# A mixture-of-experts first layer on TensorE: float32r operands in two parts in place of bf16 operands in three

## The chip, the core and the metric

The kernel runs on one core of a Trainium2 chip. The metric is the device time of one execution in microseconds (us), as the median of several executions. The core has TensorE (matrix products into PSUM banks), VectorE, ScalarE (activations), GpSimd and SyncE, which issues the DMAs here. Each runs its own program; they meet only at semaphores.

## The reference, cut to what matters

Eight batches of 1056 tokens (1024 image tokens and 32 text tokens) of width 64 go through a tokenizer, one attention block and one feed-forward block. Only the last concerns the change. It takes the normed tokens `x` and adds, over eight experts, a gated two-layer network:

```python
def step(acc, params):
    w1, bb1, w2, bb2, we = params
    h = jax.nn.gelu(xf @ w1 + bb1, approximate=False)
    y = h @ w2 + bb2
    return (acc + we[:, None] * y, None)
out, _ = jax.lax.scan(step, jnp.zeros_like(xf), (W1, b1, W2, b2, cw.T))
```

`W1` is 8 x 64 x 128, `W2` is 8 x 128 x 64, and `cw` holds the two largest softmax gates of each token and zero for the other experts. The inputs and the result are fp32.

## The kernel before, in words

The program has two phases. Phase 1 does the tokenizer and the attention, one batch in each "slot", with the steps of neighbouring batches placed beside a slot's 99 attention units (`run_phase1`). Batches go in four pairs; a tile of 128 partitions holds the 64 channels of both batches of a pair. Phase 2 (`run_phase2`, from line 1142 on) is the feed-forward block. It goes over four pairs, in each over two batches, three chunks of 352 tokens (`chunk[c]`) and four pairs of experts (`k`): 24 steps for each pair of batches, 96 in all. The order is written out by hand, the same for all engines.

The first layer has to keep more of the mantissa than bf16 holds, so both operands are cut into three bf16 parts, and six products of parts are summed. A contraction is over 64 channels only, so two parts are stacked on the 128 partitions and one matmul does two products. `w01`, `w10`, `w20` are the weights' stacks, `x01` and `x02` those of the tokens. One expert and chunk is three matmuls of 128 rows x 128 columns on 352 tokens (line 1329). They go into one of the banks 0 to 3.

In a step, TensorE does this: it waits for the gelu that frees the bank, does the three matmuls of two experts (`product`, six matmuls), and then the second layer of the step before it (`experts_out`, line 1317): two fp32 matmuls of 128 rows x 64 columns on 352 tokens, one into the lower and one into the upper half of bank 4 or 5. The trace shows each fp32 matmul as two pairs of a weight load and a matmul. ScalarE does the two gelus (line 1285), VectorE multiplies the result with the gates (line 1304), GpSimd adds up (lines 1267 and 1273). After some of the steps, TensorE also does one of the norm's steps of the next pair (`AT_NORM`: lines 613, 436, 472, 624 and, after VectorE has chosen the gates, the transposes of line 630), and the fold of a finished batch (line 1347).

The three parts of the tokens are made once for each pair, among the norm's steps: part 0 is ScalarE's copy (line 508), then VectorE subtracts (line 583), casts (line 586) and subtracts again (line 589). These three stand in VectorE's order at steps 10, 11 and 12, between the operations that choose the gates (`CHOOSE`, lines 516 to 536, three at each of the steps 10 to 15). SyncE copies the parts to the stacks with four DMAs for each batch (`stack`, line 1213), ahead of the gates' DMAs for the first batch (`load_gates`, line 1220).

The weights' parts are made by seven VectorE operations in the last attention slot, at the units `AT_SPLIT` (lines 968 to 981). In phase 1 the tokens' parts share their tiles with the parts of queries and keys (`qk_part`).

Of the kernel before, what the change touches and what calls it, by code (L numbers as in the profile page):

```python
# [4 lines left out]

F32 = mybir.dt.float32
BF16 = mybir.dt.bfloat16
I32 = mybir.dt.int32
ALU = mybir.AluOpType
ACT = mybir.ActivationFunctionType  # L10
# [51 lines left out]
X_EARLY = 14  # L62
AT_LOAD = {"first": [2 + 3 * k for k in range(X_DMAS - X_EARLY)], "load": [30 + 3 * k for k in range(X_DMAS)]}
AT_FFN = 60
AT_SPLIT = [4, 10, 16, 22, 28, 34, 40]

def max_order():

# [50 lines left out]
def build(nc, x, txt, tok_w, w_qkv, w_proj, b_proj, gate_w, gate_b, w1, b1, w2, b2, consts, out):  # L119
    with ExitStack() as ctx:  # L120
# [26 lines left out]
        gate_sb = sb("gate_sb", [P, E])  # L147
        gate_bias = sb("gate_bias", [P, E])
        w1_sb = sb("w1_sb", [P, E, HID])
        w01, w10, w20 = [sb(name, [P, E, HID], BF16) for name in ("w01", "w10", "w20")]  # L150
        w2_sb = sb("w2_sb", [P, E, D])
        biases = sb("biases", [P, E + E // 2])
        b1_sb, b2_sb = biases[:, 0:E], biases[:, E:E + E // 2]
# [9 lines left out]
        roots = sb("roots", [P, 2 * KT + 2])  # L163
        root_work = sb("root_work", [P, 2, 2 * KT + 2])

        qk_part = x_part = [sb(f"part{i}", [P, L], BF16) for i in range(3)]
        x_rest = sq

        TILES = 2 * KT + 2
        gate_pair = sb("gate_pair", [P, 2, E])  # L170
# [153 lines left out]

        FIRST_NORM = {57: [("centre", 0)], 59: [("centre", 1)], 61: [("centre", 2)], 64: [("roots", 0)],
                      67: [("scale", 0)], 69: [("scale", 1)], 71: [("scale", 2)], 74: [("gates", 0)],
                      76: [("split", 0), ("choose", 0)], 79: [("split", 1), ("choose", 1)],
                      82: [("split", 2), ("choose", 2)], 84: [("choose", 3)], 86: [("choose", 4)],
                      88: [("choose", 5)], 92: [("turn", 0)]}


# [142 lines left out]
                                            ident[0:n, 0:n], start=True, stop=True)  # L474
            return last

        X_STACKS = 4
        KPB = NCH * E
        YPB = KPB // 2
        NORM_FILLS = 2 * NCH + 3  # L480
# [14 lines left out]
        def norm_scalar(act, name, i, p):  # L495
            if name == "centre":
                if i == 0:
                    at_least(act, x_split, 3 * p)
                act.wait_ge(norm_full, NORM_FILLS * p + i + 1)
                src = norm_bank(p, i)[:, 0:CH]  # L500
                nc.scalar.activation(xc[:, chunk[i]], src, ACT.Copy)
                nc.scalar.activation(sq[:, chunk[i]], src, ACT.Square).then_inc(norm_read, 1)
            elif name == "gates":

                act.wait_ge(norm_read, NORM_FILLS * p + GATES)
                for stacks in x_stacked:
                    at_least(act, stacks, 16 * X_STACKS * p)
                nc.scalar.activation(x_part[0][:, :], xn[:, :], ACT.Copy).then_inc(x_part0, 1)
            elif (name, i) == ("choose", 1):
                act.wait_ge(gate_step, CHOICE * p + 2)  # L510
                nc.scalar.activation(gate_e[:, :, :], gate_e[:, :, :], ACT.Exp).then_inc(gate_exp, 1)
# [27 lines left out]
        def norm_vector(dve, name, i, p):  # L539
# [12 lines left out]
            elif name == "scale":  # L552
                fill, tokens = ROOTS + 1 + i, wide[i]
                dve.wait_ge(norm_full, NORM_FILLS * p + fill + 1)
                v.tensor_tensor(xn[:, tokens], xc[:, tokens],
                                norm_bank(p, fill)[:, 0:tokens.stop - tokens.start], ALU.mult)\
                  .then_inc(norm_read, 1)
            elif name == "gates":
                dve.wait_ge(norm_full, NORM_FILLS * p + GATES + 1)
                bank = norm_bank(p, GATES)  # L560
                for bp in range(2):
                    v.tensor_tensor(logits[:, KT * bp:KT * bp + KT, :],
                                    bank[:, 0:P].rearrange("p (t b e) -> p b t e", b=2, e=E)[:, bp],
                                    gate_bias[:, :].unsqueeze(1).broadcast_to([P, KT, E]), ALU.add)
                v.tensor_tensor(logits[0:TXT, 2 * KT:TILES, :],
                                bank[0:TXT, P:P + 2 * E].rearrange("p (b e) -> p b e", e=E),
                                gate_bias[0:TXT, :].unsqueeze(1).broadcast_to([TXT, 2, E]), ALU.add)\
                  .then_inc(norm_read, 1)
            elif name == "choose":

                if i == 0:
                    dve.wait_ge(norm_read, NORM_FILLS * p + GATES + 1)
                for j in range(3 * i, min(3 * i + 3, CHOICE)):
                    if j > 0:
                        dve.wait_ge(gate_step, CHOICE * p + j)
                    if j == 13:
                        dve.wait_ge(gate_exp, p + 1)
                    CHOOSE[j]().then_inc(gate_step, 1)
            elif name == "split":

                if i == 0:
                    dve.wait_ge(x_part0, p + 1)
                    ins = v.tensor_tensor(x_rest[:, :], xn[:, :], x_part[0][:, :], ALU.subtract)  # L583
                elif i == 1:
                    dve.wait_ge(x_split, 3 * p + 1)
                    ins = v.tensor_copy(x_part[1][:, :], x_rest[:, :])
                else:
                    dve.wait_ge(x_split, 3 * p + 2)
                    ins = v.tensor_tensor(x_part[2][:, :], x_rest[:, :], x_part[1][:, :], ALU.subtract)  # L589
                ins.then_inc(x_split, 1)  # L590
            elif name == "turn":

                dve.wait_ge(norm_full, NORM_FILLS * p + TURN + 1)
                at_least(dve, cw_stored, 16 * 3 * p)
                bank = norm_bank(p, TURN)
                v.tensor_copy(cw_t[:, :], bank[:, 0:P])
                v.tensor_copy(cw_tail[:, :], bank[0:2 * E, P:P + TXT]).then_inc(norm_read, 1)
# [79 lines left out]
        with nc.Block() as block:  # L677
# [173 lines left out]
            def _(dve):  # L851
# [106 lines left out]
                def attend_unit(b, par, u, g):  # L958
# [1 line left out]
                        return  # L960


                    rest = qk_rest[:, 0:E * HID].rearrange("p (e n) -> p e n", e=E)
                    low, high = slice(0, D), slice(D, P)
                    v = nc.vector
                    step = AT_SPLIT.index(u)
                    at_least(dve, w_split, step)
                    if step == 0:
                        ins = v.tensor_copy(w01[:, :, :], w1_sb[:, :, :])
                    elif step == 1:  # L970
                        ins = v.tensor_tensor(rest, w1_sb[:, :, :], w01[:, :, :], ALU.subtract)
                    elif step == 2:
                        ins = v.tensor_copy(w10[:, :, :], rest)
                    elif step == 3:
                        ins = v.tensor_tensor(w20[low, :, :], rest[low], w10[low, :, :], ALU.subtract)
                    elif step == 4:
                        ins = v.tensor_copy(w20[high, :, :], w01[high, :, :])
                    elif step == 5:
                        ins = v.tensor_copy(w01[high, :, :], w10[high, :, :])
# [8 lines left out]
            def _(pe):  # L988
# [68 lines left out]
                def side(stage, i, t, par, pair, g):  # L1057
# [100 lines left out]

        x01 = sb("x01", [P, B, L], BF16)
        x02 = sb("x02", [P, B, L], BF16)
# [9 lines left out]

        AT_NORM = {0: [("centre", 0)], 1: [("centre", 1)], 2: [("centre", 2)],
                   3: [("roots", 0)], 5: [("scale", 0)], 6: [("scale", 1)], 7: [("scale", 2)], 9: [("gates", 0)],
                   10: [("split", 0), ("choose", 0)], 11: [("split", 1), ("choose", 1)],
                   12: [("split", 2), ("choose", 2)], 13: [("choose", 3)], 14: [("choose", 4)], 15: [("choose", 5)],
                   16: [("turn", 0)]}

        FOLD_LAST, FOLD_FIRST = 8, 20
# [25 lines left out]
        with nc.Block() as block:  # L1205
            @block.sync
            def _(sp):
                def stack(b):

                    sp.wait_ge(x_split, 3 * (b // 2) + 3)  # L1210
# [99 lines left out]
            def _(pe):  # L1310
# [10 lines left out]
                def product(b, bp, c, k, n):  # L1321
                    if (c, k) == (0, 0):
                        pe.wait_ge(x_stacked[bp], 16 * X_STACKS * (n + 1))
                        if isinstance(b, int) and b == 0:
                            pe.wait_ge(w_split, 7)
# [71 lines left out]
```

## Time and profile before

| | us |
|---|---|
| Median of 3 executions (lowest to highest) | 1002.04 (996.79 to 1002.44) |
| The profiled execution, by the device's clock | 1001.97 |
| Its span from the first to the last instruction | 1000.2 |
| Phase 2, from its first matmul at 763.78 to the end | 236.4 |

The span is 1.8 us shorter than the profiled execution's time, which lies within 0.1 us of the median. Times inside the profile count from the span's start. A matmul's record runs until its result has left the array, some time after the next one may start, so what a matmul costs in a row of them is the distance between starts. "PE" rows are matmuls, "PEld" rows are the loads of the stationary operand. A shape of 64\*128 on such a row is rows (contraction) by columns of the stationary operand.

### The profile page before, as it was taken

What the parts mean: (1) busy time and instruction counts of PE and PEld (TensorE: products, weight loads), DVE (VectorE), ACT (ScalarE), POOL (GpSimd) and SP (SyncE); (2) the same over time, 40 slices, a digit from 0 to 9 for tenths busy, and PEclk for the clock granted to TensorE, in tenths of its full rate; (3) what the DMA queues carried; (4) which work ended last, traced back from release to release, by engine and by line L of the source; (5) the groups of instructions that cost most, each with busy time, mean ns of one, the idle gap of its engine ahead of it and who ended that gap; (6) DMA issues with size and microseconds to landing.
All of it is one profiled execution on the core that took longest, in us unless ns stands there. A gap on an engine that the chain in (4) does not pass through costs nothing. (4 is left out here: it accounts for less than half of the span.)

```text
span 1000.2 us, 17890 instructions
## 1 busy us (share of the span) xinstructions
PE 899.0 (90%) x5900; PEld 374.9 (37%) x5900; DVE 573.0 (57%) x1201; ACT 494.4 (49%) x1189; POOL 138.7 (14%) x148
## 2 busy tenths in 40 slices
PE   5665899999999989999999999999965989899996
PEld 5241322433342343343243334333412535354443
DVE  4025565578874557876557887788230553636331
ACT  0020254466664536665446676666533454555552
POOL 0010100011010011101001101001000344444443
PEclk9965589899999988999989999999876999999998
DMA  8329351027551005536002305100006655382731
GB/s 153 57 47 163 62 62 31 3 35 119 97 69 44 2 4 67 117 67 110 2 1 30 40 2 68 44 3 1 1 5 141 120 126 117 80 184 52 155 78 22
DMA packets 55864, 64.58 MB, mean 65 GB/s; under 512 B 23893, under 2 KB 41825, under 8 KB 55777
## 3 DMA queue, kind: packets, MB, share of 16 engines
q1 hardware_dynamic: 55777, 63.46, 35.5%
q8 instruction: 49, 0.80, 0.4%
q14 instruction: 38, 0.31, 0.1%
HBM read 36.73 MB, written 2.43 MB: 39 GB/s over the span
## 5 line engine op out<-in xcount | busy, mean ns | idle before, releaser
L887 DVE TENSOR_REDUCE max_parts<-bank 128x1 f32<-128x512 f32 x512 | 329.6, 685 | 137.4 <-PE bank L1075 134.5
L811 ACT ACTIVATE probs<-bank 128x384 f32<-128x384 f32 (+1 forms) x768 | 313.4, 466 | 191.1 <-PE bank L1038 189.6
L1038 PE MATMUL bank<-q_stack,k_stack 99*128 99x384 bf16 (+1 forms) x768 | 229.9, 329 | 4.9 <-ACT probs L811 4.2
L1075 PE MATMUL bank<-k_stack,q_stack 96*128 96x512 bf16 x512 | 208.4, 409 | 17.2 <-DMA k_stack<-part 13.2
L1016 PE MATMUL bank<-probs,v_tiles 128*32 128x384 f32 (+1 forms) x1536 | 160.2, 490 | 5.4 <-ACT heads_out L796 5.0
L1038 PEld LDWEIGHTS bank<-q_stack,k_stack 99*128 99x128 bf16 x768 | 72.2, 99 | 196.1 <-ACT probs L811 146.1
L1285 ACT ACTIVATE hid<-bank,biases 128x352 f32<-128x352 f32 x192 | 96.0, 552 | 84.8 <-PE bank L1329 84.7
L1304 DVE SCALAR_TENSOR_TENSOR prod<-bank,biases,cwb 128x352 f32<-128x352 f32 x96 | 55.8, 582 | 120.1 <-PE bank L1317 103.0
L1329 PE MATMUL bank<-x,w 128*128 128x352 bf16 (+1 forms) x576 | 105.2, 320 | 6.3 <-DMA x<-part 6.3
L1317 PE MATMUL bank<-hid,w_sb 128*64 128x352 f32 x384 | 79.2, 491 | 7.7 <-DVE prod L1304 4.0
L1052 PE MATMUL bank<-x,tok_m 128*64 128x512 f32 x256 | 68.5, 634 | 9.4 <-DMA text_in<-in_txt 8.0
L1075 PEld LDWEIGHTS bank<-k_stack,q_stack 96*128 96x128 bf16 x512 | 51.4, 101 | 64.9 <-DVE max_parts L887 20.5
L1329 PEld LDWEIGHTS bank<-x,w 128*128 128x128 bf16 x576 | 50.0, 99 | 66.9 <-ACT hid L1285 25.3
L776 POOL TENSOR_TENSOR on<-heads_out,recip 128x352 f32<-128x352 f32 x24 | 22.4, 934 | 353.2 <-ACT recip L845 353.2
L770 POOL TENSOR_TENSOR part<-qk_rest,part 128x352 bf16<-128x352 f32 x24 | 20.4, 850 | 359.5 <-DVE part L935 359.5
L1016 PEld LDWEIGHTS bank<-probs,v_tiles 128*32 128x32 f32 x1536 | 31.1, 110 | 67.2 <-ACT probs L811 42.8
L1267 POOL TENSOR_TENSOR acc<-acc,prod 128x352 f32<-128x352 f32 x48 | 48.4, 1009 | 52.9 <-DVE prod L1304 52.8
L804 ACT ACTIVATE probs_tail<-bank 128x384 f32<-128x384 f32 (+1 forms) x24 | 11.1, 463 | 55.3 <-PE bank L1034 55.2
L1267 POOL TENSOR_TENSOR acc<-prod 128x352 f32<-128x352 f32 x24 | 25.1, 1045 | 84.6 <-DVE prod L1304 84.6
L1317 PEld LDWEIGHTS bank<-hid,w_sb 128*64 128x64 f32 x384 | 19.2, 136 | 36.8 <-issue 24.1
L472 PE MATMUL bank<-cst,roots 128*64 128x128 f32 (+1 forms) x288 | 26.1, 326 | 4.6 <-DVE roots L460 4.4
L1052 PEld LDWEIGHTS bank<-x,tok_m 128*64 128x64 f32 x256 | 15.3, 141 | 35.2 <-issue 32.5
(146 smaller groups left out, 704.2 us busy)
## 6 DMA issues: line engine op xcount, KB each, us to landing
cwb<-gates_by_expert SPq DMA_DIRECT2D x16, 1056.0 KB, 12.1
x<-in_x SPq DMA_DIRECT2D x64, 256.0 KB, 6.9
q_stack<-part SPq DMA_DIRECT2D x48, 132.0 KB, 6.1
k_stack<-part SPq DMA_DIRECT2D x48, 132.0 KB, 6.6
x<-part SPq DMA_DIRECT2D x32, 132.0 KB, 2.5
h_res<-h_new SPq DMA_DIRECT2D x4, 528.0 KB, 3.0
h_all<-h_res SPq DMA_DIRECT2D x4, 528.0 KB, 3.1
h<-h_all SPq DMA_DIRECT2D x8, 264.0 KB, 3.2
```

What stands on the lines that cost most here:

```text
L472: last = nc.tensor.matmul(bank[D * bp:D * bp + D, tokens.start - WIDE * i:tokens.stop - WIDE * i], roots[0:n, 2 * t + bp:2 * t + bp + 1].b ...
L811: nc.scalar.activation(probs[:, group % 3, h, 0:n], src, ACT.Exp, scale=SCALE).then_inc(exp_done, 1)
L887: nc.vector.tensor_reduce(max_parts[:, c, H * j + h, i % 2:i % 2 + 1], src[:, :], AX.X, ALU.max)\
L1016: last = nc.tensor.matmul(o_bank[32 * h:32 * h + 32, 0:n], v_tiles[par][:, kt, h, :], probs[:, group % 3, h, 0:n], start=(kt == 0), stop=F ...
L1038: last = nc.tensor.matmul(bank[:, 0:n], ks[par][0:ROWS + 3, h, P * kt:P * kt + P], qs[par][0:ROWS + 3, h, QC[qc]], start=True, stop=True)
L1052: last = nc.tensor.matmul(bank[D * bp:D * bp + D, :], tok_m[:, part, :], xt[bp][:, first:first + NPATCH // 2, t4, :], start=(part == 0), s ...
L1075: last = nc.tensor.matmul(bank[:, :], queries(h, j), ks[par][0:ROWS, h, HALF * (i % 2):HALF * (i % 2) + HALF], start=True, stop=True)
L1267: nc.gpsimd.tensor_tensor(dst, prod[:, 0, :] if k == 1 else dst, prod[:, k, :], ALU.add)\
L1285: nc.scalar.activation(hid[:, e % 4, :], banks[e % 4][:, 0:CH], ACT.Gelu, bias=b1_sb[:, e:e + 1]).then_inc(gelu_done, 1)
L1304: nc.vector.scalar_tensor_tensor(out=prod[:, k, :], in0=banks[4 + k % 2][:, 0:CH], scalar=b2_sb[:, k:k + 1], in1=cwb[bp][:, k, chunk[c]], ...
L1317: last = nc.tensor.matmul(banks[4 + k % 2][D * o:D * o + D, 0:CH], w2_sb[:, e, :], hid[:, e % 4, :], start=True, stop=True)
L1329: last = nc.tensor.matmul(banks[e % 4][:, 0:CH], w[:, e, :], xs[:, bass.ds(b, 1), chunk[c]].rearrange("p o l -> p (o l)"), start=(i == 0), ...
```

## The change

The first layer's operands become float32r, in two parts. The weights are `w_high` (float32r, on both halves of the partitions) and `w_low` (64 partitions, the rest). The tokens are `x_part[0]` and `x_part[1]`, stacked on the two halves of `x_stack`. An expert and chunk is two matmuls: `w_high` with the whole stack, a contraction over 128 partitions, and `w_low` with the upper part alone, a contraction over partitions 0 to 63. VectorE's casts and subtractions fall from three to one for a pair's tokens and from seven to two for the weights. A batch's stack takes two DMAs in place of four, of twice the bytes each.

```diff
-AT_SPLIT = [4, 10, 16, 22, 28, 34, 40]
+AT_SPLIT = [4, 16]
...
-        w01, w10, w20 = [sb(name, [P, E, HID], BF16) for name in ("w01", "w10", "w20")]
+        w_high = sb("w_high", [P, E, HID], F32R)
+        w_low = sb("w_low", [D, E, HID], F32R)
...
-        qk_part = x_part = [sb(f"part{i}", [P, L], BF16) for i in range(3)]
-        x_rest = sq
+        qk_part = [sb(f"part{i}", [P, L], BF16) for i in range(3)]
+        x_part = [sb(f"x_part{i}", [P, L], F32R) for i in range(2)]
...
-                if i == 0:
-                    dve.wait_ge(x_part0, p + 1)
-                    ins = v.tensor_tensor(x_rest[:, :], xn[:, :], x_part[0][:, :], ALU.subtract)
-                elif i == 1:
-                    dve.wait_ge(x_split, 3 * p + 1)
-                    ins = v.tensor_copy(x_part[1][:, :], x_rest[:, :])
-                else:
-                    dve.wait_ge(x_split, 3 * p + 2)
-                    ins = v.tensor_tensor(x_part[2][:, :], x_rest[:, :], x_part[1][:, :], ALU.subtract)
-                ins.then_inc(x_split, 1)
+                dve.wait_ge(x_part0, p + 1)
+                v.tensor_tensor(x_part[1][:, :], xn[:, :], x_part[0].bitcast(F32)[:, :], ALU.subtract)\
+                  .then_inc(x_split, 1)
...
+                    if AT_SPLIT.index(u) == 0:
+                        nc.vector.tensor_copy(w_high[:, :, :], w1_sb[:, :, :]).then_inc(w_split, 1)
                     else:
-                        ins = v.tensor_copy(w10[high, :, :], w20[high, :, :])
-                    ins.then_inc(w_split, 1)
+                        dve.wait_ge(w_split, 1)
+                        nc.vector.tensor_tensor(w_low[:, :, :], w1_sb[0:D, :, :], w_high.bitcast(F32)[0:D, :, :],
+                                                ALU.subtract).then_inc(w_split, 1)
...
-                    for half, to, part in ((0, x01, 0), (1, x01, 1), (0, x02, 0), (1, x02, 2)):
-                        sp.dma_start(to[D * half:D * half + D, b, :], x_part[part][rows, :])\
+                    for part in range(2):
+                        sp.dma_start(x_stack.bitcast(F32)[D * part:D * part + D, b, :], x_part[part].bitcast(F32)[rows, :])\
                           .then_inc(x_stacked[b % 2], 16)
...
-                        for i, (w, xs) in enumerate(((w01, x01), (w10, x01), (w20, x02))):
-                            last = nc.tensor.matmul(banks[e % 4][:, 0:CH], w[:, e, :],
-                                                    xs[:, bass.ds(b, 1), chunk[c]].rearrange("p o l -> p (o l)"),
-                                                    start=(i == 0), stop=(i == 2))
+                        for i, (w, rows) in enumerate(((w_high, slice(0, P)), (w_low, slice(0, D)))):
+                            last = nc.tensor.matmul(banks[e % 4][:, 0:CH], w[rows, e, :],
+                                                    x_stack[rows, bass.ds(b, 1), chunk[c]].rearrange("p o l -> p (o l)"),
+                                                    start=(i == 0), stop=(i == 1))
```

The split steps of the two schedules (`FIRST_NORM`, `AT_NORM`) and the counts that semaphores are compared with follow these numbers.

## Rows read from the trace of the kernel before

**Rows 1.** The page, part 1: busy us, share of the span, instructions.

```profile
PE 899.0 (90%) x5900; PEld 374.9 (37%) x5900; DVE 573.0 (57%) x1201; ACT 494.4 (49%) x1189; POOL 138.7 (14%) x148
```

**Rows 2.** The chain that ended last: start us, us, what it was.

```profile
834.21 2.03 PE bank L436 x18
...
945.08 1.00 PE bank L1329 x6
946.08 0.74 PE bank L1317 x4
```

**Rows 3.** Waits, 776 to 992 us: in total, times, longest.

```profile
PE bank L630 <- DVE hit L536: 4.1, 3, 1.4
...
PE bank L1317 <- DVE prod L1304: 4.0, 4, 1.7
...
PE bank L1317 <- ACT hid L1285: 3.6, 3, 1.3
```

**Rows 4.** Windows: PE, PEld, DVE, ACT, POOL busy us (instructions), granted clock, DMA share, GB/s.

```profile
796.00:811.00 15.00, 11.63 (x68) 4.66 (x65) 14.03 (x28) 9.07 (x16) 7.75 (x7) 1.00 0.32 74
...
941.00:991.00 50.00, 47.46 (x284) 21.05 (x280) 15.18 (x26) 25.70 (x54) 25.05 (x28) 1.00 0.38 76
```

**Rows 5.** Timeline of phase 2 at 825 us, matmuls, then weight loads: start us, us.

```profile
825.12 1.07 PE L1329 MATMUL bank<-x,w 128*128 x6
826.12 0.81 PE L1317 MATMUL bank<-hid,w_sb 128*64 128x352 f32 x4
...
827.56 1.06 PE L1329 MATMUL bank<-x,w 128*128 x6
828.55 0.81 PE L1317 MATMUL bank<-hid,w_sb 128*64 128x352 f32 x4
...
825.12 0.71 PEld L1329 LDWEIGHTS bank<-x,w 128*128 128x128 bf16 x6 [0.55 <-issue]
...
827.26 0.10 PEld L1329 LDWEIGHTS bank<-x,w 128*128 128x128 bf16 x1
```

**Rows 6.** Timeline of phase 1 at 200.6 us: an fp32 matmul with a contraction over 64.

```profile
200.59 0.38 PE L1075 MATMUL bank<-k_stack,q_stack 96*128 96x512 bf16 x1
200.90 0.86 PE L1120 MATMUL bank<-xn,qkT 64*128 64x352 f32 x2
201.69 0.30 PE L1038 MATMUL bank<-q_stack,k_stack 99*128 99x288 bf16 x1
...
200.90 0.29 PEld L1120 LDWEIGHTS bank<-xn,qkT 64*128 64x128 f32 x2 [0.33 <-issue]
```

**Rows 7.** Timeline of phase 1 at 221.1 us: the same with a contraction over 128.

```profile
221.12 0.38 PE L1075 MATMUL bank<-k_stack,q_stack 96*128 96x512 bf16 x1
221.34 0.76 PE L1147 MATMUL bank<-recip_rows,cst 128*128 128x352 f32 x2
221.93 0.33 PE L1038 MATMUL bank<-q_stack,k_stack 99*128 99x384 bf16 x1
...
221.12 0.41 PEld L1147 LDWEIGHTS bank<-recip_rows,cst 128*128 128x128 f32 x2
```

**Rows 8.** VectorE: removed operations (by form: busy us, mean ns; one line: min/median/max ns).

```profile
L589 DVE TENSOR_TENSOR part<-sq,part 128x1056 bf16<-128x1056 f32 x3 | 3.7, 1248 | 0.0
...
L586 DVE CAST part<-sq 128x1056 bf16<-128x1056 f32 x3 | 2.1, 699 | 0.0
...
L969 DVE CAST w<-w_sb x1: 682/682/682, 667.3 to 667.3; 128x1024 bf16<-128x1024 f32 x1
```

**Rows 9.** Waits, 660 to 700 us: in total, times, longest.

```profile
PE bank L1097 <- DVE negm L905: 1.4, 1, 1.4
PE bank L1075 <- DVE max_parts L887: 1.0, 2, 0.6
```

**Rows 10.** Timeline at phase 2's start: SyncE's issues, and TensorE's first wait for the gates.

```profile
759.36 2.44 SPq L1213 DMA_DIRECT2D x<-part  x4
...
775.77 0.52 PE L1317 MATMUL bank<-hid,w_sb 128*64 128x352 f32 x2 [1.70 <-DVE prod L1304]
```

More of the change, by code:

```diff
@@ L7 @@
 BF16 = mybir.dt.bfloat16
+F32R = mybir.dt.float32r
 I32 = mybir.dt.int32
@@ L326, in build @@
                       67: [("scale", 0)], 69: [("scale", 1)], 71: [("scale", 2)], 74: [("gates", 0)],
-                      76: [("split", 0), ("choose", 0)], 79: [("split", 1), ("choose", 1)],
-                      82: [("split", 2), ("choose", 2)], 84: [("choose", 3)], 86: [("choose", 4)],
+                      76: [("split", 0), ("choose", 0)], 79: [("choose", 1)],
+                      82: [("choose", 2)], 84: [("choose", 3)], 86: [("choose", 4)],
                       88: [("choose", 5)], 92: [("turn", 0)]}
@@ L475, in spread_roots @@
             return last
-        X_STACKS = 4
+        X_STACKS = 2
+        X_SPLITS = 1
+        W_SPLITS = 2
         KPB = NCH * E
@@ L497, in norm_scalar @@
                 if i == 0:
-                    at_least(act, x_split, 3 * p)
+                    at_least(act, x_split, X_SPLITS * p)
                 act.wait_ge(norm_full, NORM_FILLS * p + i + 1)
@@ L960, in attend_unit @@
                         return
[L963 to L979, printed above, removed]
-                    else:
-                        ins = v.tensor_copy(w10[high, :, :], w20[high, :, :])
-                    ins.then_inc(w_split, 1)
+                    if AT_SPLIT.index(u) == 0:
+                        nc.vector.tensor_copy(w_high[:, :, :], w1_sb[:, :, :]).then_inc(w_split, 1)
+                    else:
+                        dve.wait_ge(w_split, 1)
+                        nc.vector.tensor_tensor(w_low[:, :, :], w1_sb[0:D, :, :], w_high.bitcast(F32)[0:D, :, :],
+                                                ALU.subtract).then_inc(w_split, 1)
                 run_phase1(nc.vector, attend_unit, side, lambda b, par: None, norm_vector)
@@ L1156, in build @@
         phase1.close()
-        x01 = sb("x01", [P, B, L], BF16)
-        x02 = sb("x02", [P, B, L], BF16)
+        x_stack = sb("x_stack", [P, B, L], F32R)
         cwb = [sb(f"cwb{i}", [P, E // 2, L]) for i in range(2)]
@@ L1174, in build @@
                    3: [("roots", 0)], 5: [("scale", 0)], 6: [("scale", 1)], 7: [("scale", 2)], 9: [("gates", 0)],
-                   10: [("split", 0), ("choose", 0)], 11: [("split", 1), ("choose", 1)],
-                   12: [("split", 2), ("choose", 2)], 13: [("choose", 3)], 14: [("choose", 4)], 15: [("choose", 5)],
+                   10: [("split", 0), ("choose", 0)], 11: [("choose", 1)],
+                   12: [("choose", 2)], 13: [("choose", 3)], 14: [("choose", 4)], 15: [("choose", 5)],
                    16: [("turn", 0)]}
@@ L1208, in stack @@
                 def stack(b):
-                    sp.wait_ge(x_split, 3 * (b // 2) + 3)
+                    sp.wait_ge(x_split, X_SPLITS * (b // 2 + 1))
                     rows = slice(D * (b % 2), D * (b % 2) + D)
-                    for half, to, part in ((0, x01, 0), (1, x01, 1), (0, x02, 0), (1, x02, 2)):
-                        sp.dma_start(to[D * half:D * half + D, b, :], x_part[part][rows, :])\
+                    for part in range(2):
+                        sp.dma_start(x_stack.bitcast(F32)[D * part:D * part + D, b, :], x_part[part].bitcast(F32)[rows, :])\
                           .then_inc(x_stacked[b % 2], 16)
@@ L1324, in product @@
                         if isinstance(b, int) and b == 0:
-                            pe.wait_ge(w_split, 7)
+                            pe.wait_ge(w_split, W_SPLITS)
                     for e in (2 * k, 2 * k + 1):
                         at_least(pe, gelu_done, KPB * b + E * c + e - 3)
-                        for i, (w, xs) in enumerate(((w01, x01), (w10, x01), (w20, x02))):
-                            last = nc.tensor.matmul(banks[e % 4][:, 0:CH], w[:, e, :],
-                                                    xs[:, bass.ds(b, 1), chunk[c]].rearrange("p o l -> p (o l)"),
-                                                    start=(i == 0), stop=(i == 2))
+                        for i, (w, rows) in enumerate(((w_high, slice(0, P)), (w_low, slice(0, D)))):
+                            last = nc.tensor.matmul(banks[e % 4][:, 0:CH], w[rows, e, :],
+                                                    x_stack[rows, bass.ds(b, 1), chunk[c]].rearrange("p o l -> p (o l)"),
+                                                    start=(i == 0), stop=(i == 1))
                         last.then_inc(hid_full, 1)
```

## The prediction, made before the changed kernel was run

> **What bounds the kernel now.** I read the page's busy times first: TensorE has 90% of the span, the next engine 57% [rows 1]. That is an average over two phases, and the change lives in phase 2, so the next view is the chain that ended last. There the reader is to see a pattern: 1.00 us of the first layer (line 1329, six matmuls), then 0.74 us of the second (line 1317), again and again, with the norm's and the fold's own matmuls between them [rows 2]. A step of phase 2 is therefore 1.74 us of TensorE, and 96 of them are 167 of its 236 us. The other engines have room: in the last pair, where nothing else runs, ScalarE is busy 25.7 of 50 us and VectorE 15.2, at a granted clock of 1.00, TensorE's 2.4 GHz level [rows 4]. The waits view shows where TensorE stops all the same: 4.1 us for the end of the gates' choice (three times), 4.0 for VectorE's products (four times, 1.7 of it once at the start) and 3.6 for ScalarE's gelus (three times) [rows 3]. These stand where VectorE does the choice and the splits: 14.0 of 15 us busy in such a stretch [rows 4].
>
> **What a matmul costs here.** The distance between starts counts. A bf16 matmul on 512 columns is followed by the next after 0.22 us (221.12 to 221.34) [rows 7], which is 0.43 ns a column, so 0.15 us on 352. Six are 0.90. The first layer takes 0.99 to 1.00 [rows 5], so 0.09 is left, and it lies ahead of line 1317, whose stationary operand has another shape (128\*64 after 128\*128).
>
> Two stretches of phase 1 show what such a change of shape costs. Line 1147 is an fp32 matmul of 128\*128 on 352 columns after a bf16 one of 96\*128: its load starts at once, while the matmul before still streams (221.12), and its two passes take 0.59 us to the next start [rows 7], 0.295 each. Line 1120 is the same in columns and type, but 64\*128: its load starts only at 200.90, with it, 0.31 after the matmul before instead of 0.22, and it takes 0.79 instead of 0.59 [rows 6]. So a matmul over 64 rows between matmuls over more than 64 costs 0.09 on the way in, and 0.20 more after: a first load that nothing hides, and 0.09 on the way out. That load, 128 fp32 columns, is 0.11, which a run of matmuls with next to no columns confirms (2.03 us for 18 loads and matmuls at line 436 [rows 2]). A first load of bf16 costs next to nothing: 1.00 with it exposed (load and matmul both at 825.12), 0.99 with it pulled ahead (load at 827.26, matmul at 827.56) [rows 5].
>
> **Matmuls after the change.** The four matmuls of a step now have 128, 64, 128 and 64 rows, and after them comes line 1317 with 128\*64. So every one of the four is entered and left by a change of shape. Before, there were two such changes in a step, now there are five.
>
> The stream of a float32r matmul is in no row. Fp32 takes two passes of 0.295, that is 0.59 = 4 x 0.147, as four products of half operands would; a float32r operand, already rounded to a part, needs one of the four. The bounds are the bf16 row, 0.15, and plain fp32, 0.59; one pass at fp32's rate, 0.295, is between them. I take 0.15. Its load lies between that of bf16, 0.01, and that of fp32, 0.11; I take 0.11, since its element has four bytes as fp32's has. A matmul is then 0.11 + 0.15 + 0.09 = 0.35, and the first layer of a step 4 x 0.35 = 1.40 instead of 1.00. The change of shape ahead of the first load stays in line 1317's 0.74. A step grows from 1.74 to 2.14. **96 x 0.40 = +38.4 us.** One matmul less saves less than the exposed loads and changes cost.
>
> A rule of the Trainium skill bears on the load (TensorE: Matmul & The Clock Gate, Weight-path perf modes): fast weight load is for 128 weights of a type other than fp32, and brings fp32 nothing. The rows with 0.01 and 0.11 agree for those two types; whether float32r counts as fp32 no row shows. By the fast load a step would be 1.75 and the sum that of rival 2.
>
> **What is absorbed.** With 0.4 us more in a step, ScalarE and VectorE are late less. The wait for gelus (3.6, three times, 1.2 each) comes about two steps after TensorE ran ahead, so it shrinks by 2 x 0.4 each: -2.4. The wait for products (4.0) goes: VectorE also loses a cast of 0.70 and a subtraction of 1.25 in each such stretch [rows 8], and the 1.7 us at the start are eaten by the first four steps' 1.6. The 4.1 us for the choice stay, because its last operations stand behind the product of the same step. -6.4 in all. What is late next is TensorE itself.
>
> **The other edits.** SyncE's four issues for a stack take 2.44 us [rows 10], two take half; the gates' DMA right behind them goes out 1.2 us earlier, and so does the first stack. The bytes stay the same (2 x 4 in place of 4 x 2 for each element), so I book -1.2, with 0 and -1.3 as ends. The later stacks are asked for many steps ahead. The weights' split leaves VectorE five operations fewer, of 0.68 us for the first [rows 8]; TensorE waits there for VectorE 2.4 us [rows 9]. Between 0 and -2.4, I book -1.0; were the new cast slower than the old one (1.2 instead of 0.68, the rate of a subtraction), this would be nearer to 0. ScalarE's copy of the tokens and the remaining subtraction keep their element counts: 0.
>
> **Sum.** 38.4 - 6.4 - 1.2 - 1.0 = +29.8 us, on the profiled execution's own 1001.97, which is also the median within 0.1: 1031.8, say **1032 us**, its own range 1024 to 1042.
>
> **Rivals.**
> 1. *The changes of shape cost nothing here, faster.* If the load of a 64-row matmul were pulled ahead under a 128-row one, only the first load of a step is exposed: 0.11 + 4 x 0.15 + 0.09 = 0.80 instead of 1.00, so 96 x -0.20 = -19. Waits grow back by some 1.5 in the stretches of the choice, VectorE's shorter work and the start give some 3: **981 us**. For it speaks that float32r is a type that no row has, and that no row alternates 64 and 128 rows within one accumulation. Against it speak rows 6 and 7, the same columns and type with and without. The Trainium skill has this as a rule (TensorE: Matmul & The Clock Gate, step-by-step part): a load is pulled ahead of running matmuls when row groups don't conflict or when it goes to the background buffer. By its second half this rival would hold; the trace agrees for equal shapes and disagrees at line 1120. Chance 0.09.
> 2. *Float32r weights load as fast as bf16 ones.* Then 4 x (0.01 + 0.15 + 0.09) = 1.00, nothing won or lost in a step; the other edits and VectorE's relief (2.3 of the waits, 1.2, 1.0) give **998 us**. Chance 0.12, with the loads in between.
> 3. *Float32r streams at the rate of one fp32 pass.* 4 x (0.11 + 0.295 + 0.09) = 1.98, +0.98 a step: 94 - 8.6 = +85, **1087 us**. Chance 0.07; as two passes like fp32 (4 x 0.79 = 3.16) it would be +199, **1201 us**, chance 0.02.
> 4. *The clock falls.* With 4 x 0.15 + 0.59 = 1.19 of 2.14 us streaming, the array works 56% of a step. In the stretch with VectorE's bound it streamed in six steps 6 x 1.49 = 8.9 of 15 us, 60%, and the clock stayed at 1.00 [rows 4], so I don't expect it. If a third of the steps ran at 1.2 GHz, with each stream doubled, 32 x 1.2 = +38 more: **1070 us**. Chance 0.08, half of it with so few slow steps that the time stays below 1055.
>
> **How the numbers follow.** The forecast has 0.62. The range takes it, rival 2 and the mild half of rival 4 (0.62 + 0.12 + 0.04 = 0.78, and a little of what lies near it): 995 to 1055. Left out are rivals 1 and 3 and the strong clock case. About 1% is what a measurement of this kernel can tell from no change. Faster by over 1% is rival 1 and a tail of rival 2, 0.10; within 1% the rest of rival 2, 0.11; slower the rest, 0.79.
>
> **What would show it.** In the profile after, line 1329 (under its new number) has 384 matmuls and 384 loads, half of them 64\*128, starting 0.35 us apart, each load at its matmul's start and not ahead of it, and the chain shows 1.40 and 0.74. TensorE's waits for gelus and products are nearly gone, that for the choice stays near 4. The forecast is wrong if loads of 64\*128 stand ahead of their matmuls (rival 1), if starts are 0.25 apart (rival 2) or 0.5 (rival 3), if 768 matmuls appear (fp32's two passes), or if the granted clock in the last pair is below 1.00 (rival 4).

## The result, and the profile after

The changed kernel took 1180.15 us (median, 1172.18 to 1182.71) against 1001.85 us for the kernel before in the same session, a ratio of 1.178 with a 95% interval of 1.173 to 1.184. Slower was right; 1032 us and a top of 1055 were not. The span grew by 177.5 us, from 1000.2 to 1177.7. Phase 2's first matmul comes at 761.04 instead of 763.78, so phase 1 gave 2.7 us, and phase 2 went from 236.4 to 416.7 us: +180.3.

The page of the changed kernel, part 1 and the clock line of part 2 (40 slices, in tenths of full speed):

```profile
PE 1089.2 (92%) x5708; PEld 458.5 (39%) x5708; DVE 560.5 (48%) x1188; ACT 505.0 (43%) x1189; POOL 134.9 (11%) x148
...
PEclk9955898999998999989999997566566555555555
```

The reader is to see the right end of the clock line. It stands at 5 and 6 for almost all of phase 2. Busy time alone [rows 1] would not have told: it looks like more of the same. The chain of the changed kernel in its last pair, the counterpart of [rows 2] (start us, us, what):

```profile
1113.03 2.36 PE bank L1311 x4
1115.39 1.37 PE bank L1299 x4
```

Line 1311 is now the first layer, 1299 the second. A step is 3.73 us, not 2.14. The second layer, which the change doesn't touch, also went from 0.74 to 1.37. Windows of the changed kernel, with the columns of [rows 4], one early stretch and one in the last pair:

```profile
796.00:801.00 5.00, 5.00 (x29) 3.38 (x29) 1.26 (x5) 2.50 (x4) 1.86 (x2) 1.00 0.00 0
...
1070.00:1104.00 34.00, 34.00 (x81) 14.27 (x80) 5.25 (x9) 9.42 (x17) 8.95 (x10) 0.50 0.31 64
```

The granted clock was 1.00 in the first and 0.50, that is 1.2 GHz, in the second, where it was 1.00 before [rows 4]. The first is part of one of the few short stretches of phase 2 at 1.00. In it the forecast's own terms can be checked, in the timeline of the matmuls, then of the weight loads (start us, us; compare [rows 5] and [rows 6]):

```profile
795.55 0.43 PE L1311 MATMUL bank<-x_stack,w_high 128*128 128x352 f32 x1
795.91 0.42 PE L1311 MATMUL bank<-x_stack,w_low 64*128 64x352 f32 x1
796.26 0.42 PE L1311 MATMUL bank<-x_stack,w_high 128*128 128x352 f32 x1
796.61 0.43 PE L1311 MATMUL bank<-x_stack,w_low 64*128 64x352 f32 x1
796.97 0.81 PE L1299 MATMUL bank<-hid,w_sb 128*64 128x352 f32 x4
...
795.55 0.19 PEld L1311 LDWEIGHTS bank<-x_stack,w_high 128*128 128x128 f32 x1 [0.55 <-ACT hid L1267]
795.90 0.18 PEld L1311 LDWEIGHTS bank<-x_stack,w_low 64*128 64x128 f32 x1 [0.17 <-issue]
```

Starts are 0.35 us apart, each float32r matmul is a single one (384 in all), and each load stands at its matmul's start instead of ahead. The first layer takes 1.42 at 2.4 GHz (forecast 1.40). In the last pair the same four lie 0.59 apart:

```profile
1110.41 0.66 PE L1311 MATMUL bank<-x_stack,w_high 128*128 128x352 f32 x1
1111.00 0.66 PE L1311 MATMUL bank<-x_stack,w_low 64*128 64x352 f32 x1
1111.59 1.44 PE L1299 MATMUL bank<-hid,w_sb 128*64 128x352 f32 x4
1112.96 0.66 PE L1311 MATMUL bank<-x_stack,w_high 128*128 128x352 f32 x1
```

TensorE's own waits of [rows 3] are all gone. The only one that its matmuls have left between 776 and 1170 us is this:

```profile
PE bank L1329 <- POOL acc L1255: 2.8, 1, 2.8
```

So the cost of the matmuls was forecast well at one clock, and the clock was not. Had it stayed up, phase 2 would have grown by 96 x 0.42 = 40 us less 11.7 of waits at most; between 140 and 152 of the 180 us are the clock. The question for the runs was why it fell.

### The profile page after: what moved, and what is told of

Its sections match the earlier page's. It is cut to its first block and busy times, and to the rows that moved or that the text cites. A ratio compares the mean times of both kernels' runs of the same rounds, so it can differ in the third digit from the quotient of the medians.

```text
span 1177.7 us, 17461 instructions
## 1 busy us (share of the span) xinstructions
PE 1089.2 (92%) x5708; PEld 458.5 (39%) x5708; DVE 560.5 (48%) x1188; ACT 505.0 (43%) x1189; POOL 134.9 (11%) x148
## 5 line engine op out<-in xcount | busy, mean ns | idle before, releaser
L1267 ACT ACTIVATE hid<-bank,biases 128x352 f32<-128x352 f32 x192 | 106.0, 554 | 228.8 <-PE bank L1311 227.9
L1299 PE MATMUL bank<-hid,w_sb 128*64 128x352 f32 x384 | 131.7, 785 | 0.0
L1311 PE MATMUL bank<-x_stack,w_high 128*128 128x352 f32 (+1 forms) x192 | 125.1, 652 | 6.3 <-DMA x_stack<-x_part 6.3
L1311 PE MATMUL bank<-x_stack,w_low 64*128 64x352 f32 (+1 forms) x192 | 121.5, 633 | 0.0
L1311 PEld LDWEIGHTS bank<-x_stack,w_high 128*128 128x128 f32 x192 | 53.5, 279 | 106.0 <-ACT hid L1267 53.3
L1311 PEld LDWEIGHTS bank<-x_stack,w_low 64*128 64x128 f32 x192 | 52.5, 274 | 58.7 <-issue 58.7
L1249 POOL TENSOR_TENSOR acc<-acc,prod 128x352 f32<-128x352 f32 x48 | 44.6, 929 | 136.5 <-DVE prod L1286 136.5
L1299 PEld LDWEIGHTS bank<-hid,w_sb 128*64 128x64 f32 x384 | 27.4, 196 | 28.2 <-issue 26.9
L474 PE MATMUL bank<-cst,roots 128*64 128x128 f32 (+1 forms) x288 | 30.7, 369 | 5.7 <-DVE roots L462 5.6
```

The lines of the kernel that those rows point to most:

```text
L474: last = nc.tensor.matmul(bank[D * bp:D * bp + D, tokens.start - WIDE * i:tokens.stop - WIDE * i], roots[0:n, 2 * t + bp:2 * t + bp + 1].b ...
L1249: nc.gpsimd.tensor_tensor(dst, prod[:, 0, :] if k == 1 else dst, prod[:, k, :], ALU.add)\
L1267: nc.scalar.activation(hid[:, e % 4, :], banks[e % 4][:, 0:CH], ACT.Gelu, bias=b1_sb[:, e:e + 1]).then_inc(gelu_done, 1)
L1299: last = nc.tensor.matmul(banks[4 + k % 2][D * o:D * o + D, 0:CH], w2_sb[:, e, :], hid[:, e % 4, :], start=True, stop=True)
L1311: last = nc.tensor.matmul(banks[e % 4][:, 0:CH], w[rows, e, :], x_stack[rows, bass.ds(b, 1), chunk[c]].rearrange("p o l -> p (o l)"), star ...
```

## The experiments

Eleven kernels. "Last pair" is the time between two first layers there, and the granted clock. The pad runs, grouped and the act_wait runs compute the whole result (pad128 and pad66 a little more); what the others leave out or add twice is said at each.

| run | edit | us | ratio to before (95%) | last pair |
|---|---|---|---|---|
| before | | 1001 | 1 | 1.74 us, 1.00 |
| changed | | 1180.2 | 1.178 (1.173 to 1.184) | 3.73 us, 0.50 |
| pad128 | w_low over 128 rows | 987.6 | 0.987 (0.982 to 0.992) | 1.58 us, 1.00 |
| pad66 | w_low over 66 rows | 991.3 | 0.990 (0.987 to 0.993) | 1.59 us, 1.00 |
| grouped | 128, 128, 64, 64 rows | 1104.3 | 1.104 (1.099 to 1.109) | 3.14 us, 0.50 |
| dup_both | each matmul twice | 1275.2 | 1.275 (1.269 to 1.281) | 4.91 us, 0.50 |
| bf16_alt | bf16, 128 and 64 rows in turn | 1101.9 | 1.101 (1.092 to 1.111) | 2.99 us, 0.50 |
| bf16_rows | bf16, five of six over 64 rows | 1124.2 | 1.127 (1.114 to 1.141) | 3.35 us, 0.50 |
| bf16_r66 | bf16, all six over 66 rows | 1122.1 | 1.122 (1.116 to 1.128) | 3.25 us, 0.50 |
| act_wait | pad128, gelu in 3 parts | 995.5 | 0.996 (0.994 to 0.999) | 1.58 us, 1.00 |
| act_wait4 | pad128, gelu in 4 parts | 1008.3 | 1.007 (1.003 to 1.010) | 1.79 us, 1.00 |
| act_wait5 | pad128, gelu in 5 parts | 1029.2 | 1.029 (1.023 to 1.035) | 2.11 us, 1.00 |
| cols64 | w_low over 128 rows, 64 columns | 983.1 | 0.981 (0.969 to 0.994) | 1.58 us, 1.00 |

**pad128: no change of rows.**

```diff
-        w_low = sb("w_low", [D, E, HID], F32R)
+        w_low = sb("w_low", [P, E, HID], F32R)
...
-                        for i, (w, rows) in enumerate(((w_high, slice(0, P)), (w_low, slice(0, D)))):
+                        for i, (w, rows) in enumerate(((w_high, slice(0, P)), (w_low, slice(0, P)))):
```

(and the subtraction that makes `w_low` over all partitions)

> The changed kernel with w_low made for all 128 partitions and multiplied with the whole stack, so that all four matmuls of a step are 128*128 (the fourth product of parts comes with it). Theory A (the clock falls because exposed loads and changes of shape leave the array streaming too small a share of a step): loads go ahead of their matmuls, starts 0.15 us apart, a step of 1.54 us, granted clock 1.00 in the last pair, about 982 us in all. Rival B (float32r by itself is what the clock counts as little work): the same order, but the clock stays at 0.5, a step of about 2.9 us and some 1100 us.

Measured: 987.6 us, the clock at 1.00 in the last pair. Timeline of its matmuls, then of its loads:

```profile
816.51 0.43 PE L1311 MATMUL bank<-x_stack,w_high 128*128 128x352 f32 x1
816.77 0.32 PE L1311 MATMUL bank<-x_stack,w_low 128*128 128x352 f32 x1
816.93 0.32 PE L1311 MATMUL bank<-x_stack,w_high 128*128 128x352 f32 x1
817.09 0.32 PE L1311 MATMUL bank<-x_stack,w_low 128*128 128x352 f32 x1
817.34 0.81 PE L1299 MATMUL bank<-hid,w_sb 128*64 128x352 f32 x4
...
816.61 0.19 PEld L1311 LDWEIGHTS bank<-x_stack,w_low 128*128 128x128 f32 x1
816.77 0.19 PEld L1311 LDWEIGHTS bank<-x_stack,w_high 128*128 128x128 f32 x1
```

The loads now stand 0.16 ahead of their matmuls; only the first (0.26 to the second start) is exposed. Rival B falls: float32r runs at 2.4 GHz. A start comes every 0.16 us, not every 0.15 as in bf16, which is why the step is 1.58 and not 1.54. This version beats both kernels, by 1.3% against the one before, and it computes the fourth product on top.

**grouped: fewer changes of rows.**

```diff
-                    for e in (2 * k, 2 * k + 1):
-                        at_least(pe, gelu_done, KPB * b + E * c + e - 3)
-                        for i, (w, rows) in enumerate(((w_high, slice(0, P)), (w_low, slice(0, D)))):
+                    at_least(pe, gelu_done, KPB * b + E * c + 2 * k + 1 - 3)
+                    for i, (w, rows) in enumerate(((w_high, slice(0, P)), (w_low, slice(0, D)))):
+                        for e in (2 * k, 2 * k + 1):
...
```

(the signal that a bank is full moves to each expert's `w_low` matmul; both experts' banks are now waited for at once)

> The changed kernel with both experts' w_high matmuls first and then both w_low ones (128, 128, 64, 64 rows): three changes of shape in a step instead of five, the same four matmuls. Theory A: 2 x (0.11 + 0.15 + 0.15 + 0.09) = 1.00 us for the first layer, a step of 1.75 with 68% of it streaming; the clock holds at 1.00, about 998 us. Rival B (the type): clock 0.5, a step of about 3.15, some 1130 us. Rival C (64-row matmuls count as half the work): streaming by rows is 60%, clock at least partly at 0.5, above 1050 us.

Measured: 1104.3 us. While the clock was up a step took 1.77, as expected, which is the kernel before's own cadence. But it fell to 0.50 all the same, with steps of 3.14. Theory A's forecast fails, C's comes true.

**dup_both: more streaming for the same gaps.**

```diff
-                        for i, (w, rows) in enumerate(((w_high, slice(0, P)), (w_low, slice(0, D)))):
+                        for w, rows, first, end in ((w_high, slice(0, P), True, True), (w_high, slice(0, P), True, False),
+                                                    (w_low, slice(0, D), False, False), (w_low, slice(0, D), False, True)):
...
```

> The changed kernel with every first-layer matmul issued twice, the same shape behind each other (the first w_high product is overwritten, the w_low product is added twice, so the result is a little off). Twice the first layer's streaming, the same number of exposed loads and changes of shape. Theory A: 2.0 us for the first layer, a step of 2.75 with 64% streaming; if that is enough for the clock, about 1090 us, faster than the changed kernel at 1180 with more work. If the clock stays down it is a step of 4.9 and some 1300 us, which rival B and, with its row count, rival C expect.

Measured: 1275.2 us, steps of 4.91 at clock 0.50. Filling in with more of the same matmuls doesn't bring the clock back.

**bf16_alt: the same shapes in bf16** (from the kernel before).

```diff
-                        for i, (w, xs) in enumerate(((w01, x01), (w10, x01), (w20, x02))):
+                        for i, (w, xs, rows) in enumerate(((w01, x01, slice(0, P)), (w10, x01, slice(0, D)))):
...
```

(the matmul takes `rows` of both operands; the products of `w20` and half of those of `w10` are left out)

> The kernel before with the first layer cut to two bf16 matmuls for each expert, w01 over 128 rows and w10 over 64 rows (w20 and half of w10's products are left out): the changed kernel's sequence of shapes in bf16. It prices the exposed load: starts (0.01 + 0.15 + 0.09) = 0.25 us apart instead of 0.35, a step of 1.75. Theory A: 68% of it streaming, the clock holds, about 1000 us. Rival C: as in the grouped run, the clock is partly at 0.5, above 1050 us. Rival B: the clock holds here.

Measured: 1101.9 us. The price of the load came as expected: at 2.4 GHz the four take 1.02 from the first start to line 1317,

```profile
798.94 1.08 PE L1329 MATMUL bank<-x,w 128*128 128x352 bf16 x4
799.96 0.81 PE L1317 MATMUL bank<-hid,w_sb 128*64 128x352 f32 x4
```

instead of the 1.42 of float32r, 0.10 less for each matmul: 0.01 of it is the stream (see pad128), the rest the load. The clock came otherwise: 0.50 with bf16 too. So rival B is out from the other side as well. What the runs that fell have in common so far is two things at once, matmuls over 64 rows and the changes of shape around them.

**bf16_rows and bf16_r66: many short matmuls, few gaps.** Both from the kernel before, with its six matmuls.

```diff
+                    at_least(pe, gelu_done, KPB * b + E * c + 2 * k + 1 - 3)
                     for e in (2 * k, 2 * k + 1):
-                        at_least(pe, gelu_done, KPB * b + E * c + e - 3)
...
+                            rows = slice(0, P if (e, i) == (2 * k, 0) else D)
-                            last = nc.tensor.matmul(banks[e % 4][:, 0:CH], w[:, e, :],
+                            last = nc.tensor.matmul(banks[e % 4][:, 0:CH], w[rows, e, :],
...
```

In bf16_r66 the rows are 0 to 65 for all six matmuls, and the wait for the gelus stays where it was. Both runs leave out the products on the upper rows.

> The kernel before with five of the six bf16 matmuls of a step cut to rows 0 to 63 (128, then 64 five times; the products on the upper rows are left out). At 2.4 GHz a step is 0.25 + 0.01 + 5 x 0.15 + 0.09 + 0.745 = 1.85 us, 79% of it streaming, more than in the grouped and bf16_alt runs (68%), but with fewer rows: weighted by rows it is 60%. Theory A (the clock goes by the time in which anything streams): it holds at 1.00, about 1008 us. Theory C (64-row matmuls count as half): it falls to 0.5 in the last pair as in those runs, a step of about 3.4, above 1100 us.

> The kernel before with all six first-layer matmuls of a step over rows 0 to 65 (the products on the rows above are left out): no change of shape more than before, the same cadence of 1.74 us and 84% streaming, but weighted by rows 60%, as in the bf16_rows run. Theory C in active rows: the clock falls to 0.5 in the last pair, above 1100 us. Theory C' (what counts is the shape class, so 66 rows count as 96 or 128) and theory A: it holds, about 1000 us.

Measured: 1124.2 and 1122.1 us. bf16_r66 is the cleanest of the runs. It has the matmuls, columns, types and order of the kernel before; one step of its first pair, at clock 1.00, takes 1.75 us, as before. Yet in its last pair the windows view and the chain show:

```profile
1021.00:1103.00 82.00, 82.00 (x266) 30.84 (x264) 13.18 (x23) 26.89 (x50) 21.30 (x23) 0.50 0.18 37
```

```profile
1030.45 1.87 PE bank L1329 x6
1032.33 1.37 PE bank L1317 x4
```

Six matmuls over 66 rows without a gap run at 1.2 GHz where six over 128 rows ran at 2.4 [rows 2, 4]. Theory C in active rows forecast this; C' and A had the clock hold.

**pad66: the changed kernel and two rows more.** The edit of pad128, with `slice(0, 66)` for `w_low`.

> The changed kernel with w_low's matmul over 66 rows instead of 64 (w_low made for all partitions; two rows of the low part go in with it). Nothing else differs from the changed kernel. If the change of shape goes by the 32-row steps 64 and 128, as the rows of phase 1 at 64, 96 and 99 rows have it, 66 rows are no change: loads ahead, a step of 1.58 us as in pad128 at 2.4 GHz. Theory A (share of time streaming, 74%): the clock holds, about 988 us. Theory C (active rows count): weighted by rows 1.03 of 1.58 us, 65%, above the runs that fell (59 to 60%), so it holds too or dips at times, 988 to 1010 us. Were the cause something in float32r's weights, it would stay near 1180.

Measured: 991.3 us, where 64 rows gave 1180. Timeline of its last pair:

```profile
950.90 0.43 PE L1311 MATMUL bank<-x_stack,w_high 128*128 128x352 f32 x1
951.17 0.32 PE L1311 MATMUL bank<-x_stack,w_low 66*128 66x352 f32 x1
951.33 0.32 PE L1311 MATMUL bank<-x_stack,w_high 128*128 128x352 f32 x1
```

66 rows are no change of shape after 128. With half of the first layer's matmuls short but none delayed, the clock held in the last pair and dipped more often before it than in pad128 (steps of 2.84 at places). So for the changed kernel the short matmuls alone, two of four, are not enough; together with the exposed loads and changes they are.

**act_wait, act_wait4, act_wait5: gaps, but full rows.** From pad128, each gelu is cut into three, four or five parts, so that ScalarE holds TensorE up. This is the edit for five.

```diff
-                        nc.scalar.activation(hid[:, e % 4, :], banks[e % 4][:, 0:CH], ACT.Gelu,
-                                             bias=b1_sb[:, e:e + 1]).then_inc(gelu_done, 1)
+                        for part in (slice(0, 71), slice(71, 142), slice(142, 213), slice(213, 283), slice(283, 352)):
+                            last = nc.scalar.activation(hid[:, e % 4, part], banks[e % 4][:, part], ACT.Gelu,
+                                                        bias=b1_sb[:, e:e + 1])
+                        last.then_inc(gelu_done, 1)
```

> The pad128 kernel (all four matmuls 128*128) with each gelu cut into three activations of a third of the columns each, so that ScalarE bounds a step at about 6 x 0.305 = 1.83 us and TensorE waits for it: about 65% of a step streaming, all of it with 128 rows, and no change of shape more. Theory A: no more streaming than in the grouped and bf16_alt runs (68%), so the clock falls there too, and phase 2 is longer than at 2.4 GHz. Theory C: weighted by rows it is above theirs (59%), so the clock holds at 1.00 in the last pair, with steps of 1.83 and about 1010 us.

> As act_wait, where ScalarE turned out not to bound the step (0.264 us for each third, not 0.305): each gelu in four parts of about 0.24 us, 1.92 us a step, 65% of it streaming with all rows. Theory A (time streaming): no more than grouped and bf16_alt, so the clock falls in the last pair. Theory C: the clock holds there at 1.00, steps of 1.92, about 1020 us.

> The same with five parts of about 0.225 us: 2.25 us a step, 55% of it streaming, all rows. Here theory C is below the share at which the runs with 64-row matmuls fell (59%), so both theories have the clock fall in the last pair, where ScalarE still bounds the step: about 1060 us. If it holds even here, neither share is what counts, and the changes of shape or the 64-row tile by themselves are.

Measured: 995.5, 1008.3 and 1029.2 us. The first says nothing on the question, because a third of a gelu takes 0.26 us and ScalarE didn't bound the step. The other two do: steps of 1.79 and 2.11 (1.92 and 2.25 were expected), and the clock held. The windows view of act_wait5's last pair, and its timeline:

```profile
959.00:1010.00 51.00, 41.60 (x219) 22.58 (x218) 13.42 (x23) 49.09 (x232) 21.35 (x23) 1.00 0.32 66
```

```profile
975.23 0.81 PE L1301 MATMUL bank<-hid,w_sb 128*64 128x352 f32 x4 [0.46 <-ACT hid L1268]
975.98 0.43 PE L1313 MATMUL bank<-x_stack,w_high 128*128 128x352 f32 x1
...
977.34 0.81 PE L1301 MATMUL bank<-hid,w_sb 128*64 128x352 f32 x4 [0.46 <-ACT hid L1268]
```

TensorE stands idle for 0.46 us in each step, and has 2.11 us for the four matmuls that the changed kernel gives 2.16 at 2.4 GHz. It kept its clock, where theories A and C both had it fall. So theory C as I had put it, each matmul weighted by its rows, doesn't put the runs in the right order either. Nor does it follow that the changes of shape or the 64-row tile are the cause by themselves, since bf16_r66 has neither more changes than before nor such a tile. And gaps between matmuls over full rows didn't bring down a clock that stood at 1.00.

**cols64: full rows, half the columns.** The low products of the other columns, and the high ones of these, are left out.

```diff
-                        for i, (w, rows) in enumerate(((w_high, slice(0, P)), (w_low, slice(0, D)))):
-                            last = nc.tensor.matmul(banks[e % 4][:, 0:CH], w[rows, e, :],
+                        for w, cols in ((w_high, P), (w_low, D)):
+                            last = nc.tensor.matmul(banks[e % 4][0:cols, 0:CH], w[:, e, 0:cols],
...
```

> The changed kernel with w_low's matmul over all 128 rows but only 64 of the 128 columns, overwriting instead of adding (the low products of the other columns, and the high ones of these, are left out). Shapes alternate as in the changed kernel, with full rows: 128*128, 128*64, 128*128, 128*64, and the second layer's 128*64 behind. If any change of shape costs as 128 to 64 rows does, the first layer is 0.36 + 0.29 + 0.36 + 0.20 and a step about 1.9 us at 2.4 GHz. If only active rows count for the clock, it holds at 1.00 in the last pair, about 1015 us; if halved columns count as halved rows do, or the changes by themselves, it falls, above 1100 us.

Measured: 983.1 us, clock 1.00, and nothing is lost between 128\*128 and 128\*64, 0.16 between starts:

```profile
940.32 0.42 PE L1311 MATMUL bank<-x_stack,w_high 128*128 128x352 f32 x1
940.59 0.32 PE L1311 MATMUL bank<-x_stack,w_low 128*64 128x352 f32 x1
940.75 0.32 PE L1311 MATMUL bank<-x_stack,w_high 128*128 128x352 f32 x1
940.90 0.32 PE L1311 MATMUL bank<-x_stack,w_low 128*64 128x352 f32 x1
941.16 0.81 PE L1299 MATMUL bank<-hid,w_sb 128*64 128x352 f32 x4
```

So a change from 128 rows to 64 costs, one from 128 columns to 64 doesn't, and the 0.09 ahead of the second layer is not explained by its column count, as the prediction read it: from a 128\*64 matmul to line 1299 with the same 128\*64 it is still about 0.25 (940.90 to 941.16) in place of 0.16. As the gaps didn't arise, the run can't say whether full rows with changes of shape would hold the clock; it shows only that halved columns without gaps do.

**Where the clock fell, and where it came back.** The last pair is not the whole story, since a kernel enters it with the clock that it has by then. The windows view of stretches of the earlier pairs, and of what follows, shows how each got there (columns of [rows 4]). First bf16_r66, then pad66, then act_wait5:

```profile
796.00:860.00 64.00, 64.00 (x201) 23.97 (x201) 21.01 (x42) 23.96 (x43) 17.12 (x17) 0.50 0.43 89
974.00:1118.00 144.00, 137.73 (x448) 53.45 (x448) 33.38 (x61) 46.58 (x85) 39.33 (x40) 0.50 0.24 51
...
908.00:922.00 14.00, 14.00 (x42) 6.92 (x40) 9.04 (x21) 8.79 (x15) 5.58 (x5) 0.52 0.43 97
922.00:983.00 61.00, 59.16 (x320) 32.77 (x316) 21.27 (x38) 33.70 (x71) 31.20 (x34) 1.00 0.47 95
...
802.00:808.00 6.00, 5.02 (x15) 2.49 (x16) 2.09 (x6) 5.24 (x25) 0.00 (x0) 0.50 0.04 13
809.00:839.00 30.00, 25.91 (x140) 14.65 (x136) 9.14 (x17) 29.05 (x135) 11.80 (x13) 1.00 0.69 146
```

All kernels have dips to 0.50 in phase 2, and they begin at like places: a few us behind the matmuls on 2 or 16 columns (lines 436 or 438, 621 or 624), or at or just behind a wait of TensorE of over 1 us. What differs is what follows. The kernels that kept their clock come back within 14 us, and do so while TensorE runs nothing but the two layers' steps, as pad66 does from 908 to 922. The ones that fell don't come back in such steps: bf16_r66 stays at 0.50 up to 860, and from 974 through the last pair to its end; the changed kernel does from 802 to 866 and from 898 to 1166. Before the end they rose only where the norm's matmuls (lines 610 and 474, or 613 and 472) stood between the steps. So the last pair of bf16_r66 shows that steps over 66 rows leave a low clock low, not that they bring down a high one. And act_wait5 tells nothing on a low clock with gaps, because its steps at 0.50 have none: from 804 to 809 its matmuls wait for no gelu.

## Why the prediction was wrong

- **What bounds, and which way.** Right. TensorE bounds phase 2 before and after, and one matmul less costs time.
- **The price of a matmul over 64 rows.** Right at 2.4 GHz: 0.35 us forecast, 0.35 measured; a step 2.14 and 2.16, and that at a clock that it had only in short stretches. All three choices (one pass, fp32's load, 0.09 for the change of rows) held. The stream was 0.01 longer than taken. Rivals 1, 2 and 3 are out: no load stands ahead, a matmul costs 0.10 more than in bf16, and a pass isn't 0.295. Rival 1 is what pad128 makes true, at 988 instead of 981.
- **The load of float32r.** The prediction left open whether it is bf16's or fp32's. The changed kernel and bf16_alt show it, 1.42 against 1.02 us for four matmuls, and pad128 too: 0.11 from the first load to the second (816.50 to 816.61), as for fp32. By the rule of the Trainium skill that the prediction cites (TensorE: Matmul & The Clock Gate, Weight-path perf modes), fast weight load is for types other than fp32; the traces agree with it only if float32r counts as fp32.
- **The clock: the step that failed.** The sum has no term for the clock: it takes all 96 steps at 2.4 GHz. The prediction had a lower clock as rival 4, with 0.08, and reasoned that the array streams 1.19 of 2.14 us in a step, about what it did in the stretch of the gates' choice before, at clock 1.00 [rows 4]. That comparison took each streaming matmul as equal. The matmuls of that stretch were 128 rows high; half of the new first layer is 64. The runs show that this is not the same: at the old cadence, steps over 128 rows keep the clock and steps over 66 rows stay at 0.50 (bf16_r66), while full rows with 0.46 us of idle time in a step keep 1.00 (act_wait5). For the changed kernel itself, the two rows more of pad66, which also take away the exposed loads and changes, bring 1180 us down to 991. Rival 4 was also sized too small, as a third of the steps at +1.2. The last pair's steps are all at 0.50, and a step at 1.2 GHz costs 3.73 - 2.16 = 1.57 more, since the exposed loads and changes grow too (0.59 instead of 0.35 a matmul) and the second layer takes 1.37 instead of 0.74. Over 96 steps that is 151 us.
- **What is absorbed.** -6.4 forecast; all of the 11.7 us of waits went, the choice's 4.1 too. At the lower clock a step takes TensorE longer and VectorE's operations don't, so VectorE has its choice done in time. Whether the 4.1 had stayed at 2.4 GHz this run can't show.
- **Start and phase 1.** -2.2 forecast, -2.7 measured, but the terms don't hold singly. Phase 2's first matmul comes 5.65 us after the last DMA of phase 1 was issued (755.39 to 761.04), and came 5.63 after it before (758.15 to 763.78), although the stacks' issues fell from 2.44 to 1.16 us. The -2.7 all lies in phase 1, and in pad128, whose phase 1 differs only in that `w_low` is made on 128 partitions, the first matmul came at 763.94, no earlier than before. So phase 1's part is not to be told from its own scatter.

What stays open: how much of the changed kernel's low clock is the half-empty rows and how much the exposed loads and changes of shape. It has both. Full rows with real changes of shape were not tried, since the halved columns made no gaps, and no run has gaps between full rows at 0.50. So a rival stands: that exposed loads would have kept the clock low with full rows too. Nor is it shown where the 0.09 around line 1317 comes from.

## What to carry to other kernels

Price a matmul by what stands before it: here a contraction over 64 rows between ones over 128 cost an exposed load and 0.09 us at each change, more than dropping every third matmul saved, and two more rows, or all 128, removed that. Read the granted clock of a stretch as a result of what the matmuls are, not only of how long TensorE is busy: short contractions can leave it at half, and then everything on TensorE pays, the untouched second layer included. Look also at where the clock comes back after a dip, not only at where it falls. Where rows would be left empty, try to fill them, even with a product that nobody asked for: here it was 988 us against 1180.

## What the runs showed of the hardware that I had not expected

- With the same matmuls, columns and order, the number of rows made the difference in the clock: six matmuls over 66 rows in a step ran at 1.2 GHz in the last pair (steps of 3.25), six over 128 at 2.4 (1.74).
- Dips of the clock came in all kernels. Steps over full rows, or with rows of 128 and 66 in turn (pad66), came back from them within 14 us; steps over 66 rows stayed at 0.50 for 64 us and more (bf16_r66).
- Next to 128 rows, 64 and 66 differ by far: 0.35 and 0.16 us between starts (changed kernel at 2.4 GHz, pad66).
- A change from 128 to 64 columns costs nothing between matmuls of the first layer (0.16 between starts, cols64).
- Doubling every first-layer matmul made the kernel slower still, at the same low clock (1275 us).
- Float32r with 352 columns starts every 0.16 us (pad128), bf16 every 0.15 (kernel before).
